# Finer row-maximum sets: eight queries spaced by 4, with the relative matmul trimmed on both sides

## The reference

```python
q, k, v = proj(Wq, bq), proj(Wk, bk), proj(Wv, bv)      # (16, 16 heads, 512, 8)
idx = jnp.clip(r[None, :] - r[:, None], -M, M) + M      # M = 128
content  = jnp.einsum('bhqd,bhkd->bhqk', q, k)
relative = jnp.einsum('bhqd,qkd->bhqk', q, rel_k[idx])
w = jax.nn.softmax((content + relative) / jnp.sqrt(hd), axis=-1)
```

## Time and profile before

| | us |
|---|---|
| median of 3 runs | 1658.0 |
| the three runs | 1652.87, 1658.12, 1658.0 |
| profiled execution: its span, the only time that the profile gives of it | 1623.4 |
| prologue, until the first score bank | 0 to 118.1 |
| a full turn, for example the third | 441.6 to 602.8 |
| the last turn, which makes no sets | 1250.5 to 1370.1 |
| expert stage | 1370.1 to 1623.4 |

### The profile page before, as it was taken

The page is one execution under the profiler, slowest core; times in us unless marked ns, Lnnn a source line. Parts: engine busy times, 40 slices in busy tenths (PEclk is TensorE's granted clock), DMA queues, the critical chain, the costliest instruction groups (busy, mean ns, idle before and its releaser), DMA issues.

```text
span 1623.4 us, 67801 instructions
## 1 busy us (share of the span) xinstructions
PE 1522.4 (94%) x28642; PEld 1184.3 (73%) x28642; DVE 1229.5 (76%) x3459; ACT 1112.7 (69%) x2053; POOL 472.2 (29%) x585
## 2 busy tenths in 40 slices
PE   5889999999999999999999999999999999899993
PEld 2337877787778777877777777777777776568992
DVE  7996668787878887888788878787877235644996
ACT  4437777777777777777777777777766776237881
POOL 4432020223122313231313131313101101664567
PEclk9899999999999999999999999999999999999996
DMA  3468657775565446544644464456424673425551
GB/s 85 144 189 223 149 146 165 181 184 140 113 152 110 121 110 149 111 131 100 154 103 126 104 156 98 122 112 143 97 57 102 124 207 75 121 90 150 162 167 51
DMA packets 489136, 212.10 MB, mean 131 GB/s; under 512 B 330663, under 2 KB 462436, under 8 KB 488832
## 3 DMA queue, kind: packets, MB, share of 16 engines
q1 hardware_dynamic: 474112, 165.74, 44.4%
q0 software_dynamic: 14720, 42.03, 7.5%
HBM read 105.73 MB, written 102.85 MB: 128 GB/s over the span
## 4 chain that ended last, share of the span: by engine, by line
PE 75%; DVE 15%; issue 4%; DMA 2%; ACT 1%; POOL 1%; SPq 1%; ACTq 0%; DVEq 0%; POOLq 0%
PE pv L867 14%; PE mix L822 12%; PE sc L845 9%; DVE mx L1381 8%; PE rel L874 8%; PE sc L847 7%; PE mix L824 7%; PE sc L839 4%; PE sc L1030 2%; PE rel L976 1%; POOL out_dram L1977 1%; PE sc L966 1%; PE pv L967 1%; PE mix L884 1%; ACT w L1122 1%
## 5 line engine op out<-in xcount | busy, mean ns | idle before, releaser
L1122 ACT ACTIVATE w<-sc,escale 128x512 f32<-128x512 f32 x1024 | 686.1, 688 | 310.9 <-PE sc L847 188.3
L1381 DVE TENSOR_REDUCE mx<-mix 128x1 f32<-128x512 f32 x960 | 643.3, 684 | 201.4 <-PE mix L824 191.5
L822 PE MATMUL mix<-WE 128*32 128x512 f16 (+1 forms) x1968 | 386.3, 392 | 25.0 <-DVE mx L1381 14.4
L867 PE MATMUL pv<-w,shared_part 128*9 128x128 f32 x8192 | 371.4, 273 | 3.6 <-issue 3.6
L824 PE MATMUL mix<-Wn,WE 128*32 128x384 f16 (+3 forms) x1968 | 295.2, 304 | 0.0
L845 PEld LDWEIGHTS sc<-shared_part,Wt 96*128 96x128 f16 x5120 | 223.3, 97 | 84.1 <-issue 30.9
L845 PE MATMUL sc<-shared_part,Wt 96*128 96x64 f16 x5120 | 259.0, 193 | 4.2 <-DVE mx L1381 1.9
L867 PEld LDWEIGHTS pv<-w,shared_part 128*9 128x9 f32 x8192 | 204.1, 90 | 78.2 <-issue 48.9
L874 PE MATMUL rel<-w,shared_part 128*32 128x128 f32 x5120 | 257.5, 273 | 0.6 <-issue 0.6
L847 PE MATMUL sc<-shared_part 104*128 104x128 f16 x2560 | 248.7, 219 | 1.0 <-issue 1.0
L1107 ACT ACTIVATE WE<-qp,hmask 128x256 f16<-128x256 f16 x500 | 215.6, 499 | 23.5 <-PE sc L824 23.5
(11 more groups left out here) (263 smaller groups left out, 1926.4 us busy)
## 6 DMA issues: line engine op xcount, KB each, us to landing
qm_d<-ks POOLq DMA_DIRECT2D x48, 512.0 KB, 4.5
shared_part<-qm_d SPq DMA_DIRECT2D x32, 768.0 KB
kt_d<-ks SPq DMA_DIRECT2D x48, 256.0 KB
shared_part<-kt_d SPq DMA_DIRECT2D x128, 96.0 KB
xs_d<-zrow SPq DMA_DIRECT2D x5, 2056.0 KB, 11.4
vs_d<-vst SPq DMA_DIRECT2D x16, 576.0 KB
shared_part<-vs_d SPq DMA_DIRECT2D x32, 288.0 KB
orl_d<-rel_s SPq DMA_DIRECT2D x512, 8.0 KB
```

The source lines that it names most:

```text
L822: nc.tensor.matmul(nat[rows, :], lq[:, rows], kn[b2][:, KEYS_AT[t]:KEYS_AT[t] + S], start=True, stop=False, skip_group_check=True)
L867: mm = nc.tensor.matmul(pv[b2][32 * g:32 * g + 9, P * hh:P * hh + P], VC[j][:, b2, 0 if near else 1, h, :], wt[:, :, b2, h, :], start=(j = ...
L1122: nc.scalar.activation(weights, products, ACT.Exp, scale=escale[:, 0:1]).then_inc(s["exp_done"], 1)
L1381: nc.vector.tensor_reduce(mx[:, k:k + 1], nat[:], AX.X, ALU.max).then_inc(s["mx_done"], 1)
```

## The change

The 8 queries of a set are now spaced by 4: set `k` has the queries `32 * (k // 4) + k % 4 + 4 * e`. They span 29 positions, and `near_keys` gives the range of keys for which at least one of them is not clipped: 283 columns in the middle of the sequence, fewer at its ends (156 for the first set), 244.25 in the mean over the 64 sets. The relative matmul covers this range alone. The bank's first columns are the near ones, the rest are the clipped ones. The content is now two matmuls, one over the rest from a single run of clipped copies (right ones, then left ones), and one over the near range from the plain keys. A set is thus three matmuls where it was two, and in far slots twelve where it was eight.

The order of `qp`, and with it of `qn`, `Qb` and `Qn`, follows the new numbering. The maxima of a group of 16 sets now lie in four runs of four queries for each of 8 query offsets, so `store_max` issues 8 transfers of four values a row where it had 2 transfers of 16.

```diff
-KEYS_AT = (0, P, 3 * P, 4 * P)
-NEAR_BLOCKS = ((0, 2), (0, 3), (1, 4), (2, 4))
-NEAR_OUT = (2 * P, P, 0, 0)
+RUN = 4
+GROUP_Q = NE8 * RUN
+BEYOND_R = GROUP_Q - RUN + M
+BEYOND_L = 1 - M
+EDGE = S - BEYOND_R
+RIGHT_AT, LEFT_AT, KN_W = S, S + EDGE, 2 * EDGE + S
+def near_keys(k):
+    q0 = GROUP_Q * (k // RUN) + k % RUN
+    return max(0, q0 + BEYOND_L), min(S, q0 + BEYOND_R)
...
         def store_max(n, b2, t):
-            at_least(sp, "ms_st", 32 * group)
+            at_least(sp, "ms_st", MS_STORES * group)
             for part in range(2):
-                sp.dma_start(dst[ROWS_TERM + part, t], ms[:, part, 16 * t:16 * t + 16]).then_inc(s["ms_st"], 16)
+                for g in range(P // GROUP_Q):
+                    k = 16 * t + RUN * g
+                    sp.dma_start(dst[ROWS_TERM + part, t, g], ms[:, part, k:k + RUN]).then_inc(s["ms_st"], 16)
...
             for rows in parts:
-                nc.tensor.matmul(nat[rows, :], lq[:, rows], kn[b2][:, KEYS_AT[t]:KEYS_AT[t] + S], start=True, stop=False, skip_group_check=True)
+                nc.tensor.matmul(nat[rows, rest], lq[:, rows], kn[b2][:, clipped:clipped + S - last + first], start=True, stop=True, skip_group_check=True)
             for rows in parts:
-                mm = nc.tensor.matmul(nat[rows, near], le[:, rows], Wn[:, x0:x0 + P * (last - first)], start=False, stop=True, skip_group_check=True)
+                nc.tensor.matmul(nat[rows, near], lq[:, rows], kn[b2][:, first:last], start=False, stop=False, skip_group_check=True)
+            for rows in parts:
+                mm = nc.tensor.matmul(nat[rows, near], le[:, rows], Wn[:, x0:x0 + last - first], start=False, stop=True, skip_group_check=True)
...
-                nc.scalar.activation(kn[b2][:, 3 * S // 2:2 * S], kf[:, 0, 0:S // 2], ACT.Identity, bias=kb[:, 1:2])
+                nc.scalar.activation(kn[b2][:, LEFT_AT:KN_W], kf[:, 0, 0:EDGE], ACT.Identity, bias=kb[:, 1:2])
...
-            pool.tensor_copy(qp[b2][:], qs[:, 0, :].rearrange("p (t e b) -> p e t b", t=NT, e=NE8)).then_inc(s["qsplit"], 1)
+            pool.tensor_copy(qp[b2][:].rearrange("p e (g b) -> p e g b", b=RUN), qs[:, 0, :].rearrange("p (g e b) -> p e g b", e=NE8, b=RUN)).then_inc(s["qsplit"], 1)
...
+MS_STORES = 16 * 2 * (P // GROUP_Q)
```

More of the change, by code:

```diff
@@ L194, in attention_phase @@
     Qn = [we16[:, n16 * (2 + r):n16 * (3 + r)].rearrange("p (e h k) -> p e h k", e=NE8, h=H) for r in range(2)]
-    kn = [we16[:, 4 * n16 + 2 * S * r:4 * n16 + 2 * S * (r + 1)] for r in range(2)]
-    at = (4 * n16 + 4 * S) // 2
+    kn = [we16[:, 4 * n16 + KN_W * r:4 * n16 + KN_W * (r + 1)] for r in range(2)]
+    at = (4 * n16 + 2 * KN_W) // 2
     xt = [we32[:, at + S * r:at + S * (r + 1)].rearrange("p (t d) -> p t d", t=NT) for r in range(2)]
@@ L207, in attention_phase @@
     qs = sb("qs", [P, 2, S], F16)
-    qp = [sb(f"qp{r}", [P, NE8, NT, 16], F16) for r in range(2)]
+    qp = [sb(f"qp{r}", [P, NE8, S // NE8], F16) for r in range(2)]
     ks = sb("ks", [P, 2, NT, 2, P], F16)
@@ L813, in natural @@
                 pe.wait_ge(s["qb_done"], 2 * c + k // 32 + 1)
-            t, b = k // 16, k % 16
-            lq = Qb[t // 2][:, :, :, 16 * (t % 2) + b].rearrange("p e h -> p (e h)")
+            lq = Qb[k // 32][:, :, :, k % 32].rearrange("p e h -> p (e h)")
             le = Qn[k // 32][:, :, :, k % 32].rearrange("p e h -> p (e h)")
-            first, last = NEAR_BLOCKS[t]
-            near = slice(NEAR_OUT[t], NEAR_OUT[t] + P * (last - first))
-            x0 = WN_0 - P * t - b + P * first
+            first, last = near_keys(k)
+            near, rest = slice(0, last - first), slice(last - first, S)
+            clipped = RIGHT_AT + last - BEYOND_R
+            x0 = WN_0 - (GROUP_Q * (k // RUN) + k % RUN) + first
             parts = COLUMN_TILES if tiled else WHOLE_ARRAY
             for rows in parts:
-                nc.tensor.matmul(nat[rows, :], lq[:, rows], kn[b2][:, KEYS_AT[t]:KEYS_AT[t] + S], start=True, stop=False, skip_group_check=True)
+                nc.tensor.matmul(nat[rows, rest], lq[:, rows], kn[b2][:, clipped:clipped + S - last + first], start=True, stop=True, skip_group_check=True)
             for rows in parts:
-                mm = nc.tensor.matmul(nat[rows, near], le[:, rows], Wn[:, x0:x0 + P * (last - first)], start=False, stop=True, skip_group_check=True)
+                nc.tensor.matmul(nat[rows, near], lq[:, rows], kn[b2][:, first:last], start=False, stop=False, skip_group_check=True)
+            for rows in parts:
+                mm = nc.tensor.matmul(nat[rows, near], le[:, rows], Wn[:, x0:x0 + last - first], start=False, stop=True, skip_group_check=True)
             mm.then_inc(s["nat_ps"], 1)
@@ L1104, in by_head @@
                 at_least(act, "nat_ps", 64 * (c - 1) + 32 * (half + 1))
[L1105 removed]
+            src = qp[b2][:, :, 32 * half:32 * half + 32]
             for h in heads:
[L1107 removed]
+                ins = nc.scalar.activation(Qb[half][:, :, h, :], src, ACT.Copy, scale=hmask[:, h:h + 1])
             if heads[-1] == H - 1 or (n == 0 and b2 == 0 and half == 0):
```

20 lines of the change are left out of this document (10 added, 10 removed).

## The result

| | us |
|---|---|
| before, median of 6 runs | 1658.1 (1652.9 to 1661.8) |
| after, median of 6 runs | 1842.3 (1832.0 to 1857.0) |
| ratio, 95% interval | 1.111 (1.107 to 1.115) |

The change costs 184 us; the prediction had a gain of 12. That matters here: the chips differ. On one the kernel before takes 1622 us, on two others 1656 to 1661, and 28 us of the difference lie in the expert stage. The changed kernel itself was timed beside a kernel before of 1658 us, so on a chip of the slower kind. Columns as in the earlier trace rows.

What follows compares the result with a forecast made beforehand. PE was taken to bound the kernel, with 75% of the span. Gain 21.0 - 3 (DVE) - 6 (SP) = 12 us: span 1623.4 to 1611.4, plus 34.6 to the median, forecast 1646 us, range 1632 to 1670.

Steps and rivals of the forecast that it cites:

- the columns: Relative matmul on PE: 64.3 fewer columns (26.8 ns) a near set, 94.8 fewer (39.5 ns) a far set.
- the third matmul: Content split in two on PE: 4 ns more a set, bounds 0 to 17.
- Rival C: Far sets on PE: strided tile weight loads don't hide, 30 us on the path, 1676 us; chance 0.12.
- about 85% of the sets stand on the path: Seven turns on PE: 85% of the 24.7 us saved counts, 21.0 us.
- the room of DVE: DVE idles 24.4 us before its row maxima in the third turn; 3 us taken off the gain, bounds 0 to 6.
- the SP term: SP's extra stores of maxima delay loads in the first turns only: 6 us lost, bounds 0 to 10.
- The price of a group: SP's queue: six more issues at 0.604 us, 3.6 us a group, 3.7 with gaps; 30 us per full turn.
- The slack, taken load by load: Loads behind SP's stores: later turns have 7 us against 3.7 to 7.4; turn two's keys 0.8 to 2.9 against 7.4.
- The first turns: Turn two: PE stops once for 4.5 to 6.6 us at its start; the last `oA` load costs 0 to 3 more.
- B: SP late in several places of the first turns and the last: 2 us gained, 1656 us; chance 0.17.
- A: SP's delay is covered everywhere and DVE follows fully: 21 us gained, 1637 us; chance 0.15.
- D: Sets don't stand on the path, so the change shortens nothing; chance 0.03 together with the unforeseen.

Runs made afterwards that it cites:

- the new sets with 2 stores: The changed kernel with maxima stored by 2 transfers of 16 values a row, some rows getting their neighbours' maximum; 1655.8 us, ratio 0.9988.
- 128 columns: The kernel before with its relative matmul cut to the first 128 of its 256 or 384 columns; 1626.7 us, ratio 0.980.
- six one-row stores more: The kernel before with 6 transfers of one 32-byte row to an unused place after each group's two stores of maxima; 1669.7 us, ratio 1.007.
- spacing 8: The changed kernel with queries spaced by 8 in place of 4, and 4 transfers a group in place of 8; 1696.7 us, ratio 1.023.
- spacing 8, by head: The changed kernel with queries spaced by 8, 4 stores a group, and the rows of a bank ordered head first; 1710.1 us, ratio 1.033.
- six stores 128 bytes apart: The kernel before plus 6 transfers a group of 128 rows by 4 values to an unused array, a head's query offsets 128 bytes apart; 1726.9 us, 1.043.
- six stores side by side: The kernel before plus 6 transfers a group of 128 rows by 4 values to an unused array, a head's query offsets 8 bytes apart; 1755.7 us, 1.062.
- new sets, 8 stores, old places: The changed kernel with its 8 transfers a group written where the old order of the sets puts them; 1715.3 us, ratio 1.055.
- the change, by head: The changed kernel with the rows of a bank ordered head first, same issues, packets and places in DRAM; 1878.4 us, ratio 1.132.
- GpSimd issues half: The changed kernel with 4 of each group's 8 transfers of maxima issued by GpSimd in the turns, not the prologue; 1763.4 us, ratio 1.087.
- GpSimd issues all: The changed kernel with all 8 transfers of maxima a group issued by GpSimd in the turns, not the prologue; 1706.3 us, ratio 1.052.
- the first experiment: The kernel before, its sets untouched, with each group's stores of maxima cut into 8 transfers of 4 values a row; 1760.3 us, ratio 1.061.

## Why the prediction was wrong, step by step

**Right: the columns, and nearly the third matmul.** By the trace of the new sets with 2 stores, the set of a near slot takes 380 ns in the mean over the slots of a turn, where it took 399: 19 ns less, and the prediction had 22.8. In far slots sets with 283 columns are 39 ns shorter than those with 384 and the narrower ones some 33 shorter than those with 256, 37 in the mean, where it had 35.5. A turn gains 3.3 us on PE; the prediction had 3.5. The third matmul costs some 8 ns in near slots (26.8 of columns saved, 19 seen) and some 3 in far ones, where 4 was taken. Rival C has fallen: far sets gain as much as their columns save, so the tile loads hide, and L838 starts 120 ns behind L836 there, not over 140 (12 of 333 do).

**Wrong: "about 85% of the sets stand on the path".** With 128 columns, a saving of 10.2 us a turn, 48% arrived; of the change's own 3.3 us a turn, a tenth to a third did in turns three to seven (above). The share of 85% came from the chain over a whole turn, and the room of DVE from its idle time over a whole turn, "3.5 us against 24.4 us of room". By groups of eight slots the fifth turn of the kernel before reads otherwise:

```profile
764.70:775.40 10.70, 10.61 (x246) 8.80 (x238) 9.61 (x38) 7.76 (x16) 1.01 (x1) 1.00 0.59 105
786.54:799.55 13.01, 12.81 (x288) 9.21 (x290) 8.03 (x24) 10.22 (x21) 6.98 (x11) 1.00 0.52 132
...
900.56:908.23 7.67, 7.67 (x191) 5.08 (x183) 7.17 (x18) 6.11 (x12) 2.00 (x2) 1.00 0.67 147
```

PE is full in all three, but DVE is busy for 90% of the first, 62% of the second and 93% of the last. With 128 columns the first two groups got 0.2 and 0.6 us shorter, where PE saved 0.4 and 0.9, and the last none, for 0.9. So DVE's room lies where PE's saving is not needed; that DVE is what holds PE up there is a reading of these shares and was not tested. Where the prediction had 18 us of gain, the new sets with 2 stores came out at 0.9988, some 2 us.

**Wrong, and the whole loss: the SP term, with no load late in later turns and 6 us in all, 0 to 10 as bounds.** It came out near 186 us, from 0.999 without the extra stores to 1.111 with them. Four things stand in it, the first right, the others wrong.
- The price of a group. 3.6 to 3.7 us were added for six issues at 604 ns. In turns four to seven the 64 issues of a turn take 46.8 us where 16 took 15.1: 31.7 us more, close to the 30 foretold. This part was right.
- The slack, taken load by load. Each load was given one or two stores of delay, against slack of its own. But SP waits inside its order for stores to land and for slots to come, so delay gathers over a turn; and its other issues grow as well, by some 10 us a turn. SP's issues fill this much of a turn, mean of turns four to seven, and the turn lasts:

| kernel | issues, us | turn, us | whole, ratio |
|---|---|---|---|
| before | 105.5 | 161.9 | 1 |
| six one-row stores more | 119.8 | 163.2 | 1.007 |
| spacing 8 | 122.6 | 165.4 | 1.023 |
| spacing 8, by head | 128.7 | 165.5 | 1.033 |
| six stores 128 bytes apart | 135.7 | 168.2 | 1.043 |
| six stores side by side | 137.5 | 172.5 | 1.062 |
| old sets, 8 stores | 138.8 | 173.3 | 1.061 |
| new sets, 8 stores, old places | 140.5 | 170.7 | 1.055 |
| the change | 147.3 | 185.5 | 1.111 |
| the change, by head | 153.7 | 184.4 | 1.132 |
| GpSimd issues half | 127.4 | 175.8 | 1.087 |
| GpSimd issues all | 105.6 | 166.4 | 1.052 |

The first 14 us of issues cost 1.3 us a turn, 30 to 35 cost 6 to 11. SP's issue time is not all of it: the last two rows lie above what their issues would give. "A queue that now waits a good quarter of the time" was, if anything, too low (105.5 of 161.9 us leave 35%), and the conclusion from it was wrong.
- The first turns. PE stops at turn two for 9.0 us (foretold 4.5 to 6.6), in the first experiment for 11.0, since a group of eight takes up to 9.4 us just there. The place was right. But the key loads are not the only ones: at the o loads of turn two, where 0 to 3 us were foretold, the eight slots take 30.8 us for 11.3, 25.3 in the first experiment.
- The memory. "49,152 more tiny packets are under 1% of the bytes" was true and beside the point: their place, 8 bytes side by side, is worth some 5% by itself, a term that the prediction put at nothing. No row of the kernel before could show it.

**The rivals.** B (SP late in several places, 1656) had the mechanism of the queue and under a tenth of its size; it was held down by "SP catches up in its idle stretches". A (SP's delay covered everywhere) falls with PE's stop of 9 us. D (the sets don't stand on the path) had 0.03 together with all that was unforeseen; it was too broad, since 128 columns bring 2%, but it is nearer to what the change's own saving did than the 85%. Of the prediction's two tests, "I am wrong if a turn's length doesn't fall" is what happened: turns three to seven take 180 to 190 us. SP never pausing is not: in the fourth turn it still has 4 pauses of over 2 us, together 15 us, where it had 7, together 35. So loads come late long before the queue is full.

**A slip that the ratio does not show:** 34.6 us were added to the span for the median. By what the two chips take, they belonged to another chip.

## What to carry to other kernels

Count a queue's issue time per turn before adding to it, and treat the waits within its order as fixed: here 14 us more of issues a turn made it 1.3 us longer, 30 to 35 us more 6 to 11, and 8-byte writes side by side came on top. Read how busy the other engines are in short stretches, not over a turn, before calling a share of PE's work on the path. And when a finer tiling cuts stores into runs of a few bytes, price the number of rows and the place of the runs, not the bytes.

## What the runs showed of the hardware that was not expected

- Writes of 8 bytes side by side in DRAM are dearer than the same ones apart: 1.062 against 1.043 in the separate test (128 bytes apart, one chip), 1.111 against 1.055 with the same instructions (32 bytes apart, two chips). With the neighbours one after another in a transfer it was worse still, 1.132. Packets of other transfers then take over 1 us more often (114 against 13 of 512 bytes), but their number is no price: at 1.132 there are 101.
- SP's issue is shorter for one row than for 128, and hardly goes with the bytes of a row: 250 ns for one row of 32 bytes, 566 for 128 rows of 8 bytes, 604 for 128 rows of 32 bytes. GpSimd's takes 597 for the 8-byte ones.
- Chips differ by 35 us in this program, 28 of them in the expert stage (250.6 against 278.3 us, 125 against 113 GB/s), few in the turns (807 against 812 to 815 us for turns three to seven).
